# First tile of an attention: projections taken into the score banks, ahead of the last products of the stage before

## The reference, cut to what matters

```
x  = x + banded_attention(layernorm(x), ctx, ctx)      # |i-j| <= 128 within 1024 rows
s  = layernorm(x)
for l in 0, 1:
    h = shift_token(s)                    # left half of a row, right half of the row before
    q, k, v = split(h @ wqkv[l])          # 8 heads of 64
    q, k = l2norm(q)*q_scale, l2norm(k)*k_scale
    q, k = rotary_xpos(q, k)
    o = softmax(q k^T over the last 256 rows) v
    s = s + o @ wo[l]
    h = layernorm(shift_token(s)) * ln_g + ln_b
    a, g = split(h @ w1[l] + b1[l])
    s = s + (a * gelu(g)) @ w2[l] + b2[l]
out = x + s
```

## Time and profile before

| | us |
|---|---|
| median of three runs | 3019.92 |
| the profiled execution, its own time | 3020.34 |
| its span (first to last instruction) | 3018.4 |
| PE busy | 2970.5 (98%) |
| DVE busy | 1615.1 (54%) |
| ACT busy | 1236.5 (41%) |
| POOL busy | 1134.9 (38%) |
| mean granted TensorE clock | 0.997 of full speed |

### The profile page before, as it was taken

One profiled execution on the slowest core, in us unless ns is written; L12 is line 12 of the kernel. 1 busy time (PEld: TensorE's weight loads), 2 busy tenths in 40 slices (PEclk: granted clock), 3 DMA queues, 4 the chain that ended last, 5 costly groups with the idle time before them and its releaser, 6 DMA issues. The chain is left out here.

```text
span 3018.4 us, 44260 instructions
## 1 busy us (share of the span) xinstructions
PE 2970.5 (98%) x17040; PEld 2420.2 (80%) x17040; DVE 1615.1 (54%) x3359; ACT 1236.5 (41%) x2497; POOL 1134.9 (38%) x1200
## 2 busy tenths in 40 slices
PE   7999999999999999999999999999999999999999
PEld 6787888888878888888887888888878888888887
DVE  6975667766765333333324766776675433333332
ACT  6864555555664111121123555555565212111111
POOL 6755556556631101111103556655561111211111
PEclk9999999999999999999999999999999999999999
DMA  7642111111132111001122111111114110111110
GB/s 248 199 162 73 43 40 50 57 43 45 38 108 71 44 45 45 31 20 39 44 81 72 33 43 47 50 50 43 54 57 133 57 45 31 53 55 52 45 53 30
DMA packets 144182, 190.52 MB, mean 63 GB/s; under 512 B 21335, under 2 KB 75099, under 8 KB 143973
## 3 DMA queue, kind: packets, MB, share of 16 engines
q1 hardware_dynamic: 143972, 187.70, 19.5%
HBM read 132.44 MB, written 52.46 MB: 61 GB/s over the span
## 5 line engine op out<-in xcount | busy, mean ns | idle before, releaser
L963 PE MATMUL quad<-fhT_f,w_h_f 128*128 128x512 f32 (+1 forms) x1392 | 550.9, 396 | 1.5 <-ACT w_h_f L1025 1.5
L965 PE MATMUL quad<-fhT_f,w_l_f 128*128 128x512 f32 (+1 forms) x1392 | 544.9, 391 | 0.0
L964 PE MATMUL quad<-fhT_f,w_h_f 128*128 128x512 f32 (+1 forms) x1392 | 543.4, 390 | 0.0
L1610 DVE SCALAR_TENSOR_TENSOR u_f<-quad,bias_f,gate_f_raw 128x512 f32<-128x512 f32 (+1 forms) x174 | 130.4, 750 | 698.9 <-PE quad L965 618.6
L1679 POOL TENSOR_SCALAR stats<-stats 128x1 f32<-128x1 f32 x64 | 43.4, 679 | 1020.3 <-DVE stats L1585 1019.7
L1765 POOL TENSOR_TENSOR turned_qk<-with_cos,with_sin 128x256 f32<-128x256 f32 x256 | 188.7, 758 | 457.1 <-DVE with_cos L1496 365.0
L1176 ACT ACTIVATE lprob<-lprob,small 128x384 f32<-128x384 f32 (+2 forms) x512 | 288.6, 565 | 157.3 <-DVE small L1471 157.2
L747 PE MATMUL bank_pair<-wqkv_h,hT 128*128 128x512 f32 x1024 | 330.4, 404 | 0.5 <-DVE with_sin L1496 0.5
L1277 ACT ACTIVATE gate_f_raw<-quad,bias_f 128x512 f32<-128x512 f32 (+1 forms) x174 | 119.4, 686 | 507.0 <-PE quad L965 507.0
L1025 ACT ACTIVATE uT_f<-u_f 128x512 fp32r<-128x512 f32 (+2 forms) x176 | 117.3, 666 | 511.2 <-DVE u_f L1610 511.2
L965 PEld LDWEIGHTS quad<-fhT_f,w_l_f 128*128 128x128 f32 (+1 forms) x1392 | 256.8, 184 | 63.1
(11 more groups left out here) (214 smaller groups left out, 6014.6 us busy)
## 6 DMA issues: line engine op xcount, KB each, us to landing
s_in<-stream SPq DMA_DIRECT2D x128, 128.0 KB, 2.7
s_res<-stream SPq DMA_DIRECT2D x64, 256.0 KB, 2.9
stream<-a_out SPq DMA_DIRECT2D x64, 256.0 KB, 2.0
w_h_f_raw<-in_L_ffn_w SPq DMA_DIRECT2D x60, 256.0 KB, 5.2
h_in_f<-stream SPq DMA_DIRECT2D x112, 128.0 KB, 2.5
res_f<-stream SPq DMA_DIRECT2D x47, 256.0 KB, 3.4
x_in<-in_x SPq DMA_DIRECT2D x32, 256.0 KB, 2.8
ctx_in<-in_ctx SPq DMA_DIRECT2D x32, 256.0 KB, 3.0
```

The source lines that it names most:

```text
L963: e.matmul(bank[0:n, :], high, hT[:, 0, c, :], start=c == 0, stop=False)
L964: e.matmul(bank[0:n, :], high, hT[:, 1, c, :], start=False, stop=False)
L965: ins = e.matmul(bank[0:n, :], low, hT[:, 0, c, :], start=False, stop=c == KC - 1)
L1610: e.scalar_tensor_tensor(out=Fm.u[q % 2][0:n, :], in0=up_bank(2 * (g * HC + j) + 1)[0:n, :], scalar=Fm.bias1[0:n, 0, j:j + 1], in1=Fm.gate ...
```

## The change

Five edits, made in both layers unless one is named.

1. Queries and keys of tile 0 are projected into `quad[:, 2:4]` (function `qk_banks`) instead of `bank_pair`, and before the last products of the stage before: ahead of mix(31) in the first hand-over, ahead of down(7, 10) in the second. The value projection of tile 0 comes after those products. Turning and splitting the rows of tile 0 moves forward with them.
2. Step 1 is put in another order: all 24 query and key matmuls of tile 1 first, then the rows of tile 2 are turned, and the 12 value matmuls of tile 1 are laid around turn_q(0) and turn_k(0). The squares, ropes and rotations of tile 0 move to step 0 (function `rotated_tile`), and step 1 has none. The rows of tile 3 are turned ahead of the second part of tile 2's projection.
3. In layer 1's first two steps DVE splits queries and keys before the quarters of wo, where the quarters came first.
4. In step 32 of each attention ACT copies the turned probabilities before the first two normalised tiles (`split_normalised`), not after.
5. In the first hand-over the DMAs for tile 2's rows are issued right behind tile 1's.

```diff
+    def qk_banks(t):
+        return bank_pair if t else quad[:, 2:4, :]
+    def rotated_tile(s):
+        return 0 if s == 0 else s - 1 if 2 <= s <= TILES else None
...
             attend_load(l, 1)
+            if l == 0:
+                attend_load(l, 2)
...
-                if s + 2 < TILES and (l == 0 or s):
+                if 0 < s < TILES - 2:
                     attend_load(l, s + 2)
... tensor_program, project: the waits of tile 0's queries and keys
+                    elif l:
+                        w.wait_ge(S("gate") if part else S("u"), l * GROUPS * HC - 1 + part)
                     else:
+                        w.wait_ge(S("score_max"), TILES)
... tensor_program, band
+                if s == TILES + 2:
+                    turn_first_rows(0)
                 if 0 <= s - 3 < TILES:
                     band_scores(s - 3)
...
-                if s == TILES + 2:
-                    turn_first_rows(0)
                 if s == TILES + 3:
-                    project(0, 0, 0, 12)
+                    project(0, 0, 12, 36)
... tensor_program, attend
+                if s == 0:
+                    turn_h(1)
+                    project(l, 0, 0, 12)
+                if s == 1:
+                    project(l, 1, 12, 36)
+                    turn_h(2)
+                    project(l, 1, 0, 6)
+                    turn_q(0)
+                    project(l, 1, 6, 9)
+                    turn_k(0)
+                    project(l, 1, 9, 12)
...
+                    if (s, d) == (2, 0):
+                        turn_h(3)
... tensor_program, ffn, last group
+                    if l + 1 < DEPTH and (g, j) == (GROUPS - 1, 9):
+                        turn_first_rows(l + 1)
             if l + 1 < DEPTH:
-                turn_first_rows(l + 1)
+                project(l + 1, 0, 12, 36)
             down(GROUPS - 1, FULL)
... scalar_program, attend
-                    if d == 0 and 1 <= s <= TILES:
-                        square(s - 1)
+                    if d == 0 and rotated_tile(s) is not None:
+                        square(rotated_tile(s))
...
+                    if 0 <= turned[0] < TILES:
+                        copy_turned(*turned)
                     if (s, d) == (TILES, 1):
                         split_normalised(l, 0, early_bank(0))
                         split_normalised(l, 1, early_bank(1))
-                    if 0 <= turned[0] < TILES:
-                        copy_turned(*turned)
...
+                    if (s, d) == (1, 1):
+                        keep_v(1)
... vector_program, attend: the quarters of wo move behind split_k
-                    for quarter in range(KC):
-                        if l and (s, d) == (1 + quarter // 2, 1):
-                            attend_split(l, 3, quarter)
...
                     if d and 1 <= s <= TILES:
                         split_k(s - 1)
+                    for quarter in range(KC):
+                        if l and (s, d) == (1 + quarter // 2, 1):
+                            attend_split(l, 3, quarter)
... vector_program and pool_program: rope, norm_sum, rotate, inverse_norm and
... scale_rotated take rotated_tile(s) in place of s - 1
```

More of the change, by code:

```diff
@@ L731, in project @@
                 part, (c, i) = PARTS[at // 12], divmod(at % 12, 3)
-                bank = banks[0] if part == 2 else bank_pair[:, part, :]
+                bank = banks[0] if part == 2 else qk_banks(t)[:, part, :]
                 if (c, i) == (0, 0):
@@ L889, in attend @@
                         scores(t, d)
-                    if inside and (l, s, d) > (0, 0, 0):
+                    if inside:
                         project(l, s, PROJECTED[d][0], PROJECTED[d][1])
@@ L1163, in square @@
                 w.wait_ge(S("norm_sum"), n)
-                if t == 0:
+                if t == 0 and l:
+                    w.wait_ge(S("down"), GROUP * GROUPS * HC * l)
+                elif t == 0:
                     wait_phase()
@@ L1521, in attend @@
                             maximum(t, h)
-                    if d == 0 and 1 <= s <= TILES:
-                        rope(s - 1, 0, A.with_cos, A.rope_cos, "with_cos")
-                        rope(s - 1, 0, A.with_sin, A.rope_sin, "with_sin")
-                        norm_sum(s - 1)
+                    if (s, d) == (0, 0):
+                        split_h(1)
+                    if d == 0 and rotated_tile(s) is not None:
+                        rope(rotated_tile(s), 0, A.with_cos, A.rope_cos, "with_cos")
+                        rope(rotated_tile(s), 0, A.with_sin, A.rope_sin, "with_sin")
+                        norm_sum(rotated_tile(s))
                     if early is not None:
@@ L1538, in attend @@
                                 ffn_split(l, j, third)
[L1539 to L1545 removed]
+                    if d == 0 and rotated_tile(s) is not None:
+                        rope(rotated_tile(s), 1, A.with_cos, A.rope_cos, "with_cos")
+                        rope(rotated_tile(s), 1, A.with_sin, A.rope_sin, "with_sin")
+                    if d == 0 and 1 <= s < TILES - 1:
                         split_h(s + 1)
```

70 lines of the change are left out of this document (36 added, 34 removed).

## The result

The changed kernel takes 3015.33 us (median of 20 executions, 3014.44 to 3019.88), the kernel before 3019.18 us (20 executions on the same chip, 3017.20 to 3022.05). The ratio is 0.9987 with a 95% interval of 0.9981 to 0.9992: faster by 3.9 us, 0.13%, which is less than 0.2%. The forecast was 3015.7. The profiled execution took 3016.03 us (span 3014.1) against 3020.34 (3018.4) of before.

A forecast was written before the change was run, and what follows sets the result against it. PE, 98% busy, bounds the kernel; in the hand-overs a chain over DVE and POOL ends its waits. -1.7 - 3.3 + 0.8 = -4.2 us from 3020.34 gives 3016.1, less 0.42 for the median: 3015.7 us, range 3012.0 to 3019.2.

The forecast's parts named there:

- First hand-over: Hand-over into layer 0's attention: mix(31) 1.1 us earlier, scores(0) 1.8 earlier; term -1.7 us, bounds -1.0 to -2.2.
- rival C: First hand-over: low clock after 5.1 us idle time takes its gain; total 3017.4 us; chance 0.24 together with E.
- Second hand-over: Hand-over into layer 1's attention: scores(0) 6.0 us earlier, most given back; term -3.3 us, bounds -2 to -6.
- The deduction of 0.4 for a low stretch: Second hand-over: settled -3.7 us became -3.3, for a remaining low stretch costing 0.3 to 1 us behind the waits.
- Ends of the attentions: Edit 4, both layers: turn_q(31) gains 0.95 us, but the turn of probabilities comes later; +0.4 us a layer, +0.8 in all.
- kT's low part comes 0.6 us later: End of attention: fhT reaches DVE 1.5 us later, its splits stand ahead of kT's, delaying kT's low part 0.6 us.
- Edit 5: First hand-over: earlier loads of tile 2's rows cost 0; at most 1 us if the cover fails.
- D: After the 5.1 us gap PE stays at low clock through next tiles; 10 us of it gives 3020.5; chance 0.04.
- The wait for POOL at tile 1: First hand-over, argument against C: PE waits for POOL again at tile 1, which hides a slow PE; no size given.

## Why the prediction was right

The time, 3015.33, is 0.4 us from the forecast, and the mechanism was the one worked out. By its steps:

- **First hand-over, forecast -1.7, measured -1.6 in this trace** (-1.6 to -2.4 over five kernels that are alike there). mix(31) -1.1 forecast, -1.2 measured; turn_q(0) -1.2 and -1.3; idle time 5.1 and 4.83; scores(0) -1.8 and -1.6. kT's low part was ready 2.5 us after turn_k's start, not 2.0, since the turn took 1.11 us at the low clock instead of 0.66. Two slips in the working cost nothing: the 24 + 6 matmuls that it names between mix(31) and turn_q(0) leave out tile 0's 12 values, which its time of 244.1 includes (244.3 measured, without the start's shift), and before had two more waits of PE there, 0.47 us for a rope and 0.84 us for tile 2's rows, so that the one long wait replaced five short ones and not three. That low stretch was rival C's mechanism: it was there (10.3 us), and took 1.1 us here and 0.3 to 0.5 in the four others, not all of the gain. Why it held PE's work for 10 us in one trace and for 3 to 5 in the four others, with the same instructions there, stays open.
- **Second hand-over, forecast -3.3, measured -4.0.** scores(0) -6.0 forecast; measured -6.2 with the 0.3 carried in, -5.9 without. Maxima -3.9 and -3.9; with_cos of tile 2 -3.45 and -3.7; settled -3.7 and -4.0. The deduction of 0.4 for a low stretch was wrong for this trace: the stretch came (0.62 over 4.5 us) and cost nothing, as three kernels without it (edit 5 undone, idle time filled, mix(31) in between) settle at the same -4.0; with edit 4 undone it came some 1 us earlier and the step is -3.7. One waypoint was far off and did not show in the end: the second half of tile 1's scores, forecast at -4.9 with a wait of 1.8 us for hT, comes at -6.7 with a wait of 1.46.
- **Ends of the attentions, forecast +0.8, measured 0.0.** turn_q(31) moved by the 0.95 forecast, fhT's split on DVE by 1.4 where I had 1.5; what failed is "kT's low part comes 0.6 us later": I took DVE's work between fhT and kT at its durations of before, and one of them was 0.53 us longer at its old place, beside POOL, than at its new one.
- **Edit 5, forecast 0.** On the chain it is 0, as said. That it takes away a wait after which PE had work, and with it a shorter stay at the low clock, was not foreseen: 0.3 to 1.0 us in the traces. In before, too, PE had waited for these rows inside the chain's wait, 0.84 us.
- **The sum.** The steps add to -5.6 where I had -4.2, and the medians moved by 3.9. The profiled executions differ by 4.3 because the changed one began 1.3 us late by chance. The medians' 3.9 (2.4 to 5.7 by the interval) is below 5.6, and so it is with every kernel of the table: the medians moved by 0.1 to 2.7 us less than the steps, 1.1 on average. The one trace of before, in which the start lies 0.3 us ahead of the average of the others and which took 1.2 us more than before's median, may be a long one inside; with one trace of before I can't tell. So the steps compare these kernels with each other more surely than with before, and that the forecast of the total came within 0.4 us is in part luck: two of its three terms were off by 0.7 and 0.8, both the same way.
- **Rivals.** D's 3020.5 for 10 us of low clock should read 3020.7 by its own price. The wait for POOL at tile 1, on which the case against C leaned, stands in none of the rows shown; the trace of before has it, with 0.42 us.

The rule of the Trainium skill that the prediction weighed ("TensorE: Matmul & The Clock Gate", "What's actually happening": the low clock is the default that activity lifts) is borne out in its direction by this trace: the long idle time was followed by a longer low stretch (10.3 us against 3.9), and the second hand-over, with less idle time, has a shorter one (4.5 us at 0.62, 10.4 at 0.52 before). In the four kernels that are alike in the first hand-over the stretch held PE's work for only 3 to 5 us. It did not make rival C's time.

## What to carry to other kernels

Ask of a hand-over which product its chain starts from, and put that one first: here 24 matmuls were moved ahead of the very product on which 4.8 us of table scaling and all that follows hung, and putting it earlier, or taking the scaling out of the chain, gave 1.6 to 2.4 us more there, about what the change had. Work on a side engine that waits for nothing new (tables, weight splits) belongs in the idle time ahead of the chain, not inside it. When one operation is moved ahead of another, follow what the other now stands in front of: of 6 us at the scores 2 were given back at the maxima, and splitting wo in idle time won 1.2 of them.

## What the runs showed of the hardware

- The clock fell behind short waits too: 1.94 and 1.10 us with a turn and three matmuls between them were followed by 8 us at 0.50, and 3.07 us of waiting in one piece with work on both sides by a low stretch (a turn of 1.12 us) that was over by 249.69 (0.66 us). Five kernels with the same instructions at the same place had low stretches of different lengths there (up to 10.3 us).
- What a low clock costs depends on what runs beside it: in the changed kernel's first hand-over PE lost 4.6 us by it (9.63 us at 0.52) and the kernel 1.1 us, and in its second PE lost 1.7 us (4.36 us at 0.62) and the kernel nothing.
- A pair of DVE splits with both inputs in SBUF took 1.29 us with POOL idle and 2.28 beside POOL's rotation, which went from 1.42 to 2.30; a scaling took 0.42 us, and 0.95 beside POOL's key scale.
- In twelve profiles of kernels that are alike up to x1(30) its position varies by 2.3 us (225.35 to 227.64), which is more than half of what was to be measured; positions relative to it repeat to 0.1 us where the code and the clock do not differ.
